# Attention steps of 256 queries and four heads in place of 512 queries and two heads, in a two-layer AdaLN transformer on one Trainium2 core

## The reference

```python
h = _layernorm(x) * (1 + ca) + sa
x = x + ga * L0_attn(h)         # 16 heads of 8, causal softmax, values of 32 per head, gelu, Wf
h = _layernorm(x) * (1 + cb) + sb
x = x + gb * L0_ffn(h)          # 8 experts, 2 chosen, and a shared one
...
x = x + ga * L1_attn(h)         # 6 plain heads, 4 hyperbolic, 6 with normalized q and k; rotary, causal
x = x + gb * L1_ffn(h)          # 16 experts, 4 chosen, and a shared one
...
# hyperbolic heads
arg = jnp.maximum(-curv * inner, 1.0 + 1e-07)
scores = 1.0 / (eps + jnp.sqrt(1.0 / curv) * jnp.arccosh(arg)) + causal_bias
```

## The kernel before

| engine | what, for the job started at p | position |
|---|---|---|
| PE | `hyp_scores` (L749) | p |
| DVE | `hyp_arg`: L1383, then the square L1388 | p + 1 |
| ACT | `hyp_root` (L1041, L1042) | p + 1 |
| POOL | sum (L1708) | p + 1 |
| ACT, POOL | `hyp_log` (L1047), scaling (L1704, one instruction a head) | p + 2 |
| ACT | `hyp_score` (L1052, L1053) | p + 3 |
| DVE | `hyp_shift` (L1396) | p + 3 |
| ACT, POOL, PE | `hyp_exp` (L1058), cut (L1618), `hyp_values` (L804) | p + 4 |

## Time and profile before

### The profile page before, as it was taken

One profiled execution on the slowest core, in us unless ns is written; L12 is line 12 of the kernel. 1 busy time (PEld: TensorE's weight loads), 2 busy tenths in 40 slices (PEclk: granted clock), 3 DMA queues, 4 the chain that ended last, 5 costly groups with the idle time before them and its releaser, 6 DMA issues. The chain is left out here.

```text
span 2681.4 us, 30177 instructions
## 1 busy us (share of the span) xinstructions
PE 2193.9 (82%) x10649; PEld 842.9 (31%) x10649; DVE 1505.3 (56%) x3298; ACT 1345.3 (50%) x1923; POOL 835.0 (31%) x909
## 2 busy tenths in 40 slices
PE   3799867678999886777998987767899998677789
PEld 1223332224433242222443234222343224322244
DVE  2564356676565255676655525667655544576642
ACT  1145437784234534787324454578523454367932
POOL 1012214552422212454331121355232112145534
PEclk9599876678999986668899989657799998775789
DMA  4200131102500023100420002210061002301012
GB/s 132 67 19 2 53 92 30 34 1 63 136 21 20 1 80 95 35 1 1 131 85 23 2 17 84 74 35 1 13 156 44 19 2 71 84 21 34 1 47 88
DMA packets 67847, 128.33 MB, mean 48 GB/s; under 512 B 11396, under 2 KB 24836, under 8 KB 63076
## 3 DMA queue, kind: packets, MB, share of 16 engines
q1 hardware_dynamic: 67696, 126.40, 17.0%
HBM read 109.99 MB, written 15.20 MB: 47 GB/s over the span
## 5 line engine op out<-in xcount | busy, mean ns | idle before, releaser
L1323 DVE TENSOR_REDUCE mx<-ps 128x1 f32<-128x512 f32 (+3 forms) x1248 | 639.2, 552 | 466.4 <-PE ps L663 356.2
L1069 ACT ACTIVATE pr<-ps 128x1024 f32<-128x1024 f32 (+3 forms) x672 | 515.4, 804 | 424.3 <-PE ps L733 422.1
L660 PE MATMUL ps<-kop,qop 72*128 72x512 bf16 (+6 forms) x1248 | 444.2, 378 | 134.8 <-DVE mx L1323 103.2
L733 PE MATMUL ps<-qop,kop 75*128 75x512 bf16 (+7 forms) x1344 | 405.6, 366 | 110.2 <-DVE wb L1383 41.9
L1610 POOL TENSOR_SCALAR_AFFINE_SELECT pr<-pr 128x512 f32<-128x512 f32 x224 | 146.2, 653 | 802.4 <-ACT pr L1069 801.6
L779 PE MATMUL ps<-pr,vt 128*32 128x512 f32 (+3 forms) x2688 | 346.8, 593 | 8.2 <-POOL pr L1610 7.1
L1130 ACT ACTIVATE pr<-ps 128x512 f32<-128x512 f32 x224 | 133.8, 597 | 344.9 <-PE ps L886 281.3
L660 PEld LDWEIGHTS ps<-kop,qop 72*128 72x128 bf16 (+1 forms) x1248 | 124.3, 102 | 529.8 <-DVE mx L1323 320.5
L733 PEld LDWEIGHTS ps<-qop,kop 75*128 75x128 bf16 (+1 forms) x1344 | 122.1, 105 | 342.8 <-ACT pr L1069 119.4
L896 PE MATMUL ps<-pr,w_down 128*128 128x512 f32 x384 | 197.8, 600 | 3.1 <-POOL pr L1601 3.1
L663 PE MATMUL ps<-maskqk,identb 128*128 128x128 bf16 x832 | 200.1, 248 | 0.0
(11 more groups left out here) (313 smaller groups left out, 3102.4 us busy)
## 6 DMA issues: line engine op xcount, KB each, us to landing
wb<-gates_scratch SPq DMA_DIRECT2D x192, 256.0 KB, 3.3
kop<-kparts_scratch SPq DMA_DIRECT2D x32, 576.0 KB
qop<-qparts_scratch SPq DMA_DIRECT2D x96, 192.0 KB
on<-hmax_scratch SPq DMA_DIRECT2D x8, 1024.0 KB, 5.6
kparts_scratch<-on SPq DMA_DIRECT2D x12, 256.0 KB, 2.9
qparts_scratch<-on SPq DMA_DIRECT2D x12, 256.0 KB, 4.5
qparts_scratch<-wb SPq DMA_DIRECT2D x12, 192.0 KB
kparts_scratch<-wb SPq DMA_DIRECT2D x12, 192.0 KB
```

Of the source, the lines that this page charges most:

```text
L660: mm = pe.matmul(o, qop[0:k, slot(l, u), j, qb * P:(qb + 1) * P], kop[0:k, slot(l, u), j, k0:k0 + wd], start=True, stop=not diag)
L733: mm = pe.matmul(o, kop[0:k, slot(l, u), 2 * pair + j, kb * P:(kb + 1) * P], qop[0:k, slot(l, u), 2 * pair + j, q0:q0 + wd], start=True, s ...
L1069: nc.scalar.activation(pr[:, g % 3, 2 * pair:2 * pair + 2, o0:o0 + wd], ps[:, bank:bank + 2, o0:o0 + wd], ACT.Exp).then_inc(a.exps, 1)
L1323: ins_ = nc.vector.tensor_reduce(mx[:, nth(l, u) % 2, j, qb, col % 2:col % 2 + 1], ps[:, bank, 0:wd], AX.X, ALU.max, negate=True)
```

## The change

A step now takes `QW` = 256 queries. Chunks of 256 have 2, 4, 6 and 8 steps: `NS` = 20 for each unit, 16 of them with 256 queries and 4 with 128 (steps 1, 5, 11 and 19). 8 of the 20 are on the diagonal. `DONE` = [6, 20] says after how many steps a half of 512 queries is complete. Four heads of 256 queries fill two banks, so each step is one score job and one ACTIVATE. `pr` holds six such steps in the same memory. The hyperbolic unit has 20 jobs of four heads, started at every second position. PE's pieces keep their shapes and number; they are spread over more positions.

```diff
+QW = 256
+for _c in range(N // QW):
+    for _kb in range(2 * (_c + 1)):
+        _q0 = max(_c * QW, _kb * P)
+        STEPS.append((_c, _kb, _q0, (_c + 1) * QW - _q0, _kb >= 2 * _c))
+DONE = [max(i for i, x in enumerate(STEPS) if x[0] // 2 == c) + 1 for c in range(NC)]
+PR_RING = 6
...
-HYP_POS = [1 + k for k in range(HYP_HALVES)]
+HYP_POS = [2 + 2 * k for k in range(NS)]
+HYP_ARG, HYP_LOG, HYP_SCORE, HYP_EXP = 1, 3, 4, 6
...
-            pieces(u, first, first + NS - 4)
+            pieces(u, first, first + NS - 7)
...
-        pieces(HYP_UNIT, 0, 6, (1,))
-        pieces(1, 6, 9)
-        plan[7].append(("maxima1", (HYP_UNIT, (1,))))
+        pieces(HYP_UNIT, 0, 9, (1,))
+        plan[10].append(("maxima1", (HYP_UNIT, (1,))))
+        pieces(1, 10, 15)
...
-        pieces(2, 13, 21)
+        pieces(2, 22, 35)
...
+                    o = score_banks(take_banks(), g)
+                    for j in range(4):
+                        mm = pe.matmul(o[:, j], kop[0:k, slot(l, u), j, kb * P:(kb + 1) * P],
+                                       qop[0:k, slot(l, u), j, q0:q0 + wd], start=True, stop=True)
...
-                        if s == 4:
+                        if s == DONE[0] + 1:
                             sums_out(u, 0)
-                        if s == 0 and u:
+                        if s == 1 and u:
                             sums_out(u - 1, 1)
...
-                        if hyp_at(p - 3) != NOBODY:
-                            hyp_score(hyp_at(p - 3))
+                        if hyp_at(p - HYP_SCORE) != NOBODY:
+                            hyp_score(hyp_at(p - HYP_SCORE))
...
-                    shift = hyp_at(p - 3) if l else NOBODY
-                    if l and hyp_at(p - 1) != NOBODY:
-                        hyp_arg(hyp_at(p - 1))
+                    shift = hyp_at(p - HYP_SCORE) if l else NOBODY
+                    if l and hyp_at(p - HYP_ARG) != NOBODY:
+                        hyp_arg(hyp_at(p - HYP_ARG))
...
-                    for i in range(2):
-                        j = 2 * (k % 2) + i
-                        z = hyp_z(b, k)[:, i]
+                    for j in range(4):
+                        z = hyp_z(b, k)[:, j]
                         nc.gpsimd.tensor_scalar(z, z, hyp[:, 4 + j:5 + j], HYP_EPS, ALU.mult, ALU.add).then_inc(h_lin, 1)
```

More of the change, by code:

```diff
@@ L61, in hyp_diagonals @@
 def hyp_diagonals(k):
-    return sum(STEPS[i // 2][4] for i in range(k))
+    return sum(STEPS[i][4] for i in range(k))
 def is_hyp(l, u):
@@ L125, in output_order @@
 def output_order(l):
-    outs = [(NS * u + 4 + 8 * c, u, c) for u in range(STD_UNITS[l]) for c in range(NC)]
+    outs = [(NS * u + DONE[c], u, c) for u in range(STD_UNITS[l]) for c in range(NC)]
     if l:
-        outs += [(HYP_POS[2 * (4 + 8 * c) - 1] + 5, HYP_UNIT, c) for c in range(NC)]
+        outs += [(HYP_POS[DONE[c] - 1] + HYP_EXP + 1, HYP_UNIT, c) for c in range(NC)]
     return sorted(outs)
@@ L711, in take_banks @@
                     if n >= 2:
[L712 to L716 removed]
+                        hyperbolic, i = JOBS[l][n - 2]
+                        pe.wait_ge(h_arg if hyperbolic else a.exps, i + 1)
                     return 2 * (n % 2)
@@ L763, in values @@
                     c, kb, q0, wd, diag = STEPS[s]
-                    o0 = q0 - c * CH
-                    last = kb == 4 * c + 3
+                    o0 = q0 % CH
+                    last = kb == 2 * c + 1
+                    z = probs(g)
                     if diag:
@@ L797, in hyp_values @@
                         pe.wait_ge(h_exp, k + 1)
-                    if kb == 0 and c and k % 2 == 0:
-                        pe.wait_ge(a.o_out, out_before(HYP_UNIT, c))
+                    if kb == 0 and c == 2:
+                        pe.wait_ge(a.o_out, out_before(HYP_UNIT, 1))
                     z = hyp_z(b, k)
-                    for i in range(2):
-                        j = 2 * (k % 2) + i
+                    for j in range(4):
                         h = 4 * HYP_UNIT + j
                         mm = pe.matmul(ps[32 * j:32 * j + 32, 5, o0:o0 + wd], vt[:, kb, 32 * h:32 * h + 32],
-                                       z[:, i], start=kb == 0, stop=kb == 4 * c + 3, tile_position=(0, 32 * j))
+                                       z[:, j], start=kb == 0, stop=kb == 2 * c + 1, tile_position=(0, 32 * j))
                     mm.then_inc(h_pv, 1)
@@ L1060, in std_exp @@
                 def std_exp(g):
-                    u, s = divmod(g, NS)
-                    c, kb, q0, wd, _ = STEPS[s]
-                    o0 = q0 - c * CH
-                    for pair in range(2):
-                        bank = 2 * (JOBS[l].index((False, g, pair)) % 2)
-                        act.wait_ge(a.scores, 2 * g + pair + 1)
-                        if g >= 3:
-                            act.wait_ge(a.pv, g - 2)
-                        nc.scalar.activation(pr[:, g % 3, 2 * pair:2 * pair + 2, o0:o0 + wd],
-                                             ps[:, bank:bank + 2, o0:o0 + wd], ACT.Exp).then_inc(a.exps, 1)
+                    act.wait_ge(a.scores, g + 1)
+                    if g >= PR_RING:
+                        act.wait_ge(a.pv, g - PR_RING + 1)
+                    nc.scalar.activation(probs(g), score_banks(2 * (JOBS[l].index((False, g)) % 2), g),
+                                         ACT.Exp).then_inc(a.exps, 1)
                 steps = STD_UNITS[l] * NS
```

169 lines of the change are left out of this document (74 added, 95 removed).

## The result

The changed kernel takes 2871.25 us (median of 4, 2867.24 to 2876.49) against 2675.68 us (2673.02 to 2679.08) for the kernel before in the same comparison: ratio 1.0715, 95% interval 1.0686 to 1.0744. It is 7.2% slower; the forecast was 2790, and 2871 lies above its range.

| stage, sum over the four batch elements | before | after | forecast | measured |
|---|---|---|---|---|
| layer 0 attention, first to last ones matmul | 660 | 726 | +44 | +66 |
| layer 1, hyperbolic phase (first root to last exponential) | 752 | 859 | +61 | +107 |
| layer 1, plain exponentials alone, ahead of and behind that phase | 114 | 133 | +4 | +19 |
| all else | | | 0 | -6 |

A forecast was written before the change was run, and what follows sets the result against it. PE was taken to bound layer 0 attention and ACT layer 1's hyperbolic phase. 11 us more per element in layer 0 (44) and 17 in layer 1 (68), 112 in all, took 2677.9 to 2790 us, range 2715 to 2860.

The forecast's parts named there:

- Values wait for the logarithm in layer 0: Layer 0, step 6 and unit ends: PE's values wait for ACT's logarithm of the sums, 4 + 3 times, 10 us per element.
- Finer steps, +9 us an element: Layer 0, PE's own work: a unit takes 28.9 us instead of 26.6, 9 us more per batch element.
- Piece waits 8 to 5 us a unit, -9 an element: Layer 0: PE's waits for pieces, mostly due to DVE, fall to about 5 us a unit instead of 8.
- the upper bound: Layer 0: 18 us more per element, if the pieces wait as before.
- ACT saves 8 us in layer 1: Layer 1 hyperbolic phase: 24 hyperbolic instructions and about 9 exponentials fewer, each worth 0.24 us, save 8 us per element.
- Chain of shift and argument, 32 + 17 us: Layer 1: ACT's root waits while DVE does shift, argument and square, 32 us; side jobs between add 17, per element.
- an upper bound of +30: Layer 1: 30 us more per element, if pieces hold hyp_scores on PE up as well.
- 10 us of other idle time in the phase: Layer 1 hyperbolic phase: of ACT's 35 us idle, 10 are left, with the late cuts.
- 1 us behind the phase: Layer 1, behind the hyperbolic phase: 1 us more per element.
- One wait only: Rival: layer 0's logarithm wait is hidden by piece waits, only layer 1 slows, 2746 us; chance 0.13.
- faster: Rival: finer steps let engines run ahead, -8 in layer 1 and -6 in layer 0 per element, 2622 us; chance 0.10.
- The clock falls in layer 0: Rival: new gaps put a tenth of layer 0 at 1.2 GHz, 15 us more per element, 2850; chance 0.14 (clock or pieces).

The follow-up runs named there:

- the earlier sums: Changed kernel with layer 0's logarithm and reciprocal of the sums one step earlier: 2811 us, ratio 1.0504.
- late shift: Changed kernel with DVE's shift of a hyperbolic job one position later, behind the next job's argument and square: 2823 us, ratio 1.0558.
- the run that was to measure them: Changed kernel with all side jobs of an even position ahead of the shift on DVE: 2854 us, ratio 1.0650.
- all four edits: Changed kernel with layer 0's logarithm of the sums one step earlier and layer 1's shift, root and values one position later: 2655 us, ratio 0.9914, the fastest kernel.
- the late logarithm: Kernel before with layer 0's logarithm and reciprocal of the sums one step later: 2761 us, ratio 1.0321; the changed kernel also has it late.
- the slowest's: Kernel before with DVE's shift ahead of the argument and square of the later job: 2858 us, ratio 1.0664.

## Why the forecast was right in kind and short in size

- **Values wait for the logarithm in layer 0: right.** 7 times, 10.0 us in all, as forecast (1.58 us at a seventh step, 1.15 at a unit's start, for 1.5 and 1.3). Its price on the stage was 11.8 us (13.5 on average over the four elements).
- **Finer steps, +9 us an element: too high.** A bare step costs 1.54 us as forecast. But with the earlier sums PE is busy 4.0 us more than before (153.8 for 149.8), not 9. Part of it is that the narrow ones take 865.41 - 865.08 = 0.33 us when scores follow, not the 0.51 that the forecast took from the earlier trace rows (821.64 to 822.15, the last 0.11 of them idle); that steps with pieces pay less, as a piece already stands between scores and values, is likely but not shown.
- **Piece waits 8 to 5 us a unit, -9 an element: wrong.** This is the failed step of layer 0. The forecast took the 28 us left over by its price list for waits. In the trace PE is idle for 163.2 - 149.8 = 13.4 us, and its waits for the maxima are 7.3 us, not 24; there was less to save. They went to 4.9. So with the sums put right the stage is still 3 to 6 us longer than before, where 11 - 10 = 1 was forecast. The number of the upper bound, 18 if the pieces wait as before, came in the second element (17.6), but not by the pieces: finer steps 4.0 and the clock 5.5 in busy time, and 8.1 more idle time, mostly the 10.0 of the new wait.
- **ACT saves 8 us in layer 1:** 4.2. There are 33 instructions fewer, as counted, but a whole hyperbolic one takes 1.06 us, and not the 0.96 with which the saving was worked out.
- **Chain of shift and argument, 32 + 17 us: right in kind, wrong in its working.** ACT waits 60.6 us for the square. 53.1 of them fall to the 18 jobs that were priced at 49; the other 7.5 (4.33 and 3.17) fall to the first two, which have no shift ahead and had no price. **This is the step that failed:** the wait was priced from VectorE's queue alone, with `hyp_scores` taken to be there in time, and a late `hyp_scores` stood only as an upper bound of +30. The runs show a second path to the same argument of nearly the same length, through GpSimd's sum and mask and PE's values: with no shift ahead at all (late shift) 55.6 us of root waits stayed and DVE waited 22.0 us for `hyp_scores`. That the sum of 18 jobs came out near is in part luck, as in the tenth job above the argument waits for the scores and not for the shift. The 17 us for side jobs stay open: the run that was to measure them moved them to another place of the same chain.
- **10 us of other idle time in the phase:** 5.1 (65.7 - 60.6). So the phase was missed by 3.8 us of ACT's own work and 11.6 of root waits, less these 4.9, in the second element.
- **1 us behind the phase:** 4.4 an element (15.0 to 19.4). After the last hyperbolic exponential there are 13 steps with 3072 queries, where 7 steps with 2816 stood. With all four edits it is still 18.5 us, so the order does not explain this part; the smaller and more numerous steps probably do.
- **The sum.** Over four elements the stages took more than forecast by 22 us in layer 0, 46 in the phase and 15 ahead of and behind it, and all else 6 less: 77, which is what the 186 us between the two spans exceed the 109 of the table by (the text of the forecast has 112, as it rounded 16.3 to 17 an element). The medians lie 196 us apart, 10 more than the spans: the profiled execution of the kernel before was longer than its median run (span 2681.4, median time 2675.7), that of the changed kernel was not (2867.2 and 2871.3).
- **Rivals.** "One wait only" and "faster" did not come. "The clock falls in layer 0" came beside the forecast: 0.95, so about a tenth of the stage's time at the lower level. Its price was 5.5 us, not 15: the forecast put a tenth of the work at half speed, which would take two tenths of the time. From 0.99 to 0.95 some 14 us more are at the lower level (0.04 x 2 x 181), and they can cost at most half of that, 7. By the Trainium skill (TensorE: Matmul & The Clock Gate, A second HAM failure mode: psum-queue depth-cycling) short idle times between groups make the clock swing; the pair of kernels with and without the late logarithm (0.95 and 0.99, 0.92 and 0.99) agrees. By the same page of the Trainium skill, Back-to-back issue gap, 2.5 ns for each of 96 more matmuls would add some 0.24 us a unit. The rows gave 2.3, and the measured busy time is 1.0, so both missed it.

## What to carry to other kernels

When steps are cut in half, every offset written in positions is half as long in time: count for each stage what work now stands between its input being issued and its use, on every engine, not only on the one that was busy longest. If an engine waits and the wait stays when its named cause is removed, there is a second path about as long; follow it in the timeline until it closes, and remove both before judging either. When work is moved to another place, look whether it has only come to stand ahead of another link of the same chain. Price waits from the recorded idle time, and not from what a price list leaves over. On each engine, put an instruction that still has to wait behind those that are ready and that others wait for.

## What was not expected of the hardware

Seven gaps of 1.4 us on average (1.8 at most) in a stage of 163 to 183 us brought the granted clock from 0.99 to 0.92 in the kernel before and, for the changed one, to 0.95, and the lower clock cost about half as much as the gaps (5.5 us for 10.0) or as much as the gaps themselves (10.9). In layer 1, where the clock of the phase lies between 0.51 and 0.71 in every kernel here, the time does not follow the clock: the fastest kernel's phase (178 us on average) has 0.57 in the second element, the slowest's (226 us) 0.64.
